# Layer 3's results turned by VectorE in 32x32 squares instead of by TensorE

## The chip, the cores and the metric

The kernel runs on one core of one Trainium2 chip. The metric is the device time of one execution in microseconds. The profile comes from one further execution that the hardware profiler recorded. Its span is shown beside the times.

## What is computed

The input x has the shape (2, 8, 256, 256): batch b, expert or channel e, row n, column d. Four blocks follow one another, each added to x: a normalisation over pairs of channels (four groups), then an expert MLP, a 3x3 convolution over channels with binarised weights, and two more expert MLPs. The MLP of an expert is what matters here:

```
h   = einsum('bend,edh->benh', gn(x), w1) + b1      # d = 256 -> h = 1024
h   = gelu(h)
out = einsum('benh,ehd->bend', h, w2) + b2          # h = 1024 -> d = 256
x   = x + out
```

There are three such layers of 8 experts (the convolution stands between the first two). The last one, whose results are the output, is called layer 3 below, after the reference.

## The kernel before

Activations lie transposed in SBUF: XT holds d on the 128 partitions (two halves c), and for each expert e and batch b the 256 rows n along the free dimension. From the second MLP layer on, the partitions hold d in an interleaved order: within each half c of 128 values, partition 2 i + g holds d = 128 c + 64 g + i, with GROUPS = 2 values of g and SPAN = 64 values of i. Every product is made in a split of three terms (high x high, high x low, low x high) for float32 accuracy, so a stationary or moving operand exists as a high part, written by ScalarE, and a low part, written by VectorE.

The three layers are 24 experts E (0 to 23), the work of one being a pass; two of them are halved, so there are 26 passes. A pass has eight units t, one for each 128 of the 1024 hidden values. In a unit TensorE makes G1 for unit u (`g1`, line 1079, six matmuls of 128x512) and then the second product of unit u - 2 (`g2`, lines 1099, 1100 and 1104, six matmuls into the ACC banks). ScalarE applies gelu to G1 (HR, line 637) and rounds it (Hh, line 641); VectorE subtracts (Hl, line 816). In between both split the weights of the next expert (lines 619 and 797, one chunk of eight in each unit), and VectorE normalises the next input (XN, line 804; Xl, line 810). At t = 2 of the next pass VectorE evicts the finished ACC banks and adds the bias and the residual (`evict`, line 830). In layer 3 this goes to XFIN, which has two slots by the parity of E. Each engine works through its own queue in order, written out by hand in one loop over the units.

XFIN holds d on partitions, but the output wants rows n on partitions. For this, in the pass after expert E of layer 3 (E from 16 to 22), TensorE transposes XFIN in four 128x128 blocks for b = 0 behind unit t = 4 and for b = 1 behind t = 6 (`out_transpose`, line 1162), into the PSUM bank TR. ScalarE copies TR to OUTT behind its t = 5 and t = 7 (`out_evac_step`, line 671), and undoes the interleaving in that copy. It waits for the store of the expert before to have left OUTT. VectorE's `evict` waits for the transposes of the expert two before (line 824). Then the SP queue stores OUTT (`store_out`, line 514), in rows of 256 values, 1 KB. In SP's queue the store for b = 0 stands behind the load of W1 of a later expert and the store for b = 1 behind the load of W2 (lines 516 to 522). The loads wait until the raw weight buffer has been split (lines 420 and 430).

The last expert (E = 23, pass FINAL) is done otherwise: `final_g2` (line 1131) makes it with rows on partitions, in two banks, one for each b. ScalarE (line 718) and VectorE (line 1014) copy them to OUTT, once the store of expert 6 from the same half of OUTT has landed, and two stores end the kernel.

Of the kernel before, what the change touches and what calls it, by code (L numbers as in the profile page):

```python
# [21 lines left out]
F32 = mybir.dt.float32  # L22
# [6 lines left out]
PART = 128  # L29
# [12 lines left out]

GROUPS = 2
SPAN = PART // GROUPS

KS = 3
ROWS = PART // C
# [54 lines left out]
def evicted_by(p):  # L102

    return DC * (p + 1)
# [147 lines left out]
def build(nc, x, w1, b1, w2, b2, cw, cb, out):  # L252
# [3 lines left out]
    with ExitStack() as ctx:  # L256
        def sb(name, shape, dt=F32, where=ctx):
            return where.enter_context(nc.sbuf_tensor(name, shape, dt))
# [4 lines left out]
        def sem(name):  # L263
            return ctx.enter_context(nc.semaphore(name))
# [57 lines left out]
            NAT = sb("NAT", [PART, NPAIR, B, 2, NC, D], F32, use)  # L322
        with ExitStack() as use:
            XFIN = sb("XFIN", [PART, 2, DC, B, N], F32, use)
            OUTT = sb("OUTT", [PART, B, NC, D], F32, use)
        XC = sb("XC", [PART, B, NBLK, NP])

        HR = sb("HR", [PART, 2, TOK])
# [32 lines left out]
        cn_done, chi, clo, conv_mm, cadded = (sem("cn_done"), sem("chi"), sem("clo"), sem("conv_mm"), sem("cadded"))  # L361
        mean_fixed = sem("mean_fixed")
        x2_in = [sem(f"x2_in{b}") for b in range(B)]
        out_tr, out_evac = sem("out_tr"), sem("out_evac")
        final_in, final_done, final_dve = sem("final_in"), sem("final_done"), sem("final_dve")
        out_st = [sem(f"out_st{b}") for b in range(B)]

# [33 lines left out]
        def evacuated(i):  # L401

            return (in_evac_dve, i // 2 - 2) if i % 2 == 0 else (in_evac_act, i // 2 + 3)

        def same_slot(p):

# [5 lines left out]
        def _(sp):  # L412
# [95 lines left out]
            def store_out(e, b, n):  # L508

                if e == C - 1 and b == B - 1:  # L510
                    sp.wait_ge(final_dve, 1)
                else:
                    sp.wait_ge(out_evac, 2 * n - 1 + b)
                sp.dma_start(out[b, e].rearrange("(c p) d -> p c d", p=PART), OUTT[:, b]).then_inc(out_st[b], 16)

            for e in range(C):
                load_w1(2 * C + e)
# [6 lines left out]
                for b in range(B):  # L524
                    store_out(e, b, e + 1)
            for b in range(B):
                sp.wait_ge(out_st[b], 16 * C)


        @block.gpsimd  # L530
# [57 lines left out]
        def _(act):  # L588
# [74 lines left out]
                    nc.scalar.dma_start(XT[GROUPS * i + g:GROUPS * (i + n):GROUPS, c, :, b],  # L663
                                        XC[j * C:(j + n) * C, b, own.stop - 1, 1:N + 1]).then_inc(x2_in[b], 16)

            def out_evac_step(E, b):

                n = E - 2 * C
                act.wait_ge(out_tr, 2 * n + b + 1)
                wait(act, out_st[b], 16 * n)  # L670
                nc.scalar.activation(OUTT[:, b].rearrange("p r (c g i) -> p (r c) g i", c=DC, g=GROUPS),
                                     TR[:].rearrange("p (a i g) -> p a g i", i=SPAN, g=GROUPS), ACT.Copy
                                     ).then_inc(out_evac, 1)

            for f in range(LAYERS):
                nc.scalar.dma_start(bias1_rows[:, f, :], b1[f].rearrange("e (t p) -> (e t) p", p=PART)
                                    ).then_inc(bias_in, 16)
# [17 lines left out]
            for u in range(UNITS):  # L695
                p, t = divmod(u, HT)
                E = PASSES[p][0]
                if u == unit(PC, 0):
                    for q in range(B * TILES):
                        conv_high(q)  # L700
                        if q >= BEHIND:
                            give_back(q - BEHIND)
                        if q == FIRST["round"]:
                            x_hi(PC, 0)
                    for q in range(B * TILES - BEHIND, B * TILES):
                        give_back(q)
                gelu(u)
                for weight in WEIGHTS_AT.get(u, ()):
                    w_hi(*weight)
                if u in SPLIT_AT:  # L710
                    x_hi(*SPLIT_AT[u])
                if E == 1 and t % 2 == 0:
                    x_evac(8 + t)
                if E > 2 * C and t in (5, 7):
                    out_evac_step(E - 1, (t - 5) // 2)
            act.wait_ge(final_done, 1)
            act.wait_ge(out_st[0], 16 * (C - 1))
            nc.scalar.activation(OUTT[:, 0].rearrange("p r d -> p (r d)"), ACC[FINAL % 2][0][:], ACT.Copy
                                 ).then_inc(out_evac, 1)


# [1 line left out]
        def _(dve):  # L723
# [95 lines left out]
            def evict(p, bs=None):  # L819
                E, bs = PASSES[p][0], bs or PASSES[p][1]  # L820
                f, e = divmod(E, C)
                dve.wait_ge(g2_done, HT * (p + 1))
                if f == LAYERS - 1:
                    wait(dve, out_tr, 2 * (E - 2 * C) - 2)
                own = slice(bs[0], bs[-1] + 1)
                cols = slice(0, width(p)) if len(bs) == len(PASSES[p][1]) else slice(bs[0] * N, (bs[-1] + 1) * N)
                for m in range(DC):
                    at = XT[:, m, e, own]
                    dst = XFIN[:, E % 2, m, own] if f == LAYERS - 1 else at
                    nc.vector.scalar_tensor_tensor(dst, acc(p, m)[:, cols].rearrange("p (b n) -> p b n", n=N),  # L830
                                                   BT2[:, f, e, m:m + 1], at, ALU.add, ALU.add).then_inc(evicted, 1)

            def add_final_bias():

# [122 lines left out]
            for u in range(UNITS):  # L957
                p, t = divmod(u, HT)
                E = PASSES[p][0]
                for J in jobs_at("aggregate", u):  # L960
                    if JOBS[J][3]["sums"] != u:
                        aggregate(J)
                if u == unit(PC, 0):
                    conv_low(0)
                    for q in range(B * TILES):
                        if q + 1 < B * TILES:
                            conv_low(q + 1)
                        conv_add(q)
                        beside_tile(q)
                if t == 2 and p > 0 and p != PC:  # L970
                    evict(p - 1)
                for J in jobs_at("sums", u):
                    if "early" in JOBS[J][3]:
                        sums(J, (1,))
                        aggregate(J)
                h_lo(u)
                for weight in WEIGHTS_AT.get(u, ()):
                    w_lo(*weight)
                for J in range(NJOBS):
                    e, bs, of, steps = JOBS[J]  # L980
                    if steps.get("early") == u:
                        sums(J, (0,))
                    if steps.get("sums") == u and "early" not in steps:
                        if u == 8:
                            for i in (7, 8):
                                dve.wait_ge(*evacuated(i))
                        sums(J)
                        if steps["aggregate"] == u:
                            aggregate(J)
                    if steps.get("mean") == u:  # L990
                        deviate(J)
                    if steps.get("eps") == u:
                        add_eps(J)
                    if steps.get("scale") == u:
                        scale_shift(J)
                        for b in range(B):
                            if J == LAST_CONV_JOB[b]:
                                to_partitions(b)
                if u + 1 in SPLIT_AT:
                    norm(*SPLIT_AT[u + 1])  # L1000
                if u in SPLIT_AT:
                    x_lo(*SPLIT_AT[u])
                if u == unit(FINAL - 1, 6):
                    add_final_bias()
                if E == 1 and t % 2 == 1:
                    x_evac(8 + t)
                if E == 1 and t == 6:
                    signs_and_means()
                    bias_of_next()
                if E == 2 and t in (2, 4, 6):  # L1010
                    band(t // 2 - 1)
            dve.wait_ge(final_done, B)
            dve.wait_ge(out_st[B - 1], 16 * (C - 1))
            nc.vector.tensor_copy(OUTT[:, B - 1].rearrange("p r d -> p (r d)"), ACC[FINAL % 2][B - 1][:]
                                  ).then_inc(final_dve, 1)


# [1 line left out]
        def _(pe):  # L1019
# [132 lines left out]
                                           xx[:, q % ring, 0:w, kh:kh + N], start=i == 0, stop=i == len(parts) - 1)  # L1152
                ins.then_inc(conv_mm, 1)

            def out_transpose(E, b):
                n = E - 2 * C
                pe.wait_ge(evicted, evicted_by(len(PASSES) - EXPERTS + E))
                wait(pe, out_evac, 2 * n + b)
                for r in range(NC):
                    for c in range(DC):  # L1160
                        at = r * D + c * PART
                        ins = nc.tensor.transpose(TR[:, at:at + PART], XFIN[:, E % 2, c, b, r * PART:(r + 1) * PART],  # L1162
                                                  ident[:])
                ins.then_inc(out_tr, 1)

            pe.wait_ge(consts, 3)
            stay_busy(5)
            for i in range(4):
# [18 lines left out]
            for u in range(UNITS):  # L1187
# [26 lines left out]
                    variance_over_partitions(J)  # L1214
                if E == 1:
                    x_transpose(8 + t)
                if E > 2 * C and t in (4, 6):
                    out_transpose(E - 1, t // 2 - 2)
            for u in (UNITS - 2, UNITS - 1):
                final_g2(u)  # L1220

# [24 lines left out]
```

## Time and profile before

| | before |
|---|---|
| median of 3 runs | 608.18 us (605.89 to 608.58) |
| profiled execution | 611.48 us, span 609.7 us |
| TensorE, matmuls | 592.4 us busy, 97% |
| VectorE | 426.7 us busy, 70% |
| ScalarE | 419.1 us busy, 69% |
| DMA, hardware queue of SP | 54262 packets, 70.31 MB, 37.9% of 16 engines |

The span is the time from the first to the last instruction of the profiled execution; the time of the execution contains it. A busy share is an average over the whole span. The profile cuts the span in 40 slices of 15.2 us; layer 3 fills the last 12 of them. A timeline row gives the start, the duration, the engine and line, and in square brackets how long the engine had been idle and what ended that.

### The profile page before, as it was taken

Reading aid. Unit: us, or ns where it says so; the run is one execution under the profiler, and the core shown is the slowest. Engines: PE = TensorE matmul, PEld = TensorE weight load, DVE = VectorE, ACT = ScalarE, POOL = GpSimd, SP = SyncE. Lnnn points to the kernel's source line nnn. Section 1 sums busy time; section 2 is a strip of 40 time slices with the busy share of each in tenths; the row PEclk is TensorE's granted clock in tenths of the full one; section 3 lists DMA queues with packets and bytes.
Section 4 is the critical chain, followed back from the end, with each engine's and each line's share of the span. In section 5 each row is a group of like instructions: output and inputs, shape, how many; then the busy total and the mean of one; then the engine's idle time right before and its main releaser. Section 6 shows DMA issues by size and latency. Waiting matters only on the chain.

```text
span 609.7 us, 8604 instructions
## 1 busy us (share of the span) xinstructions
PE 592.4 (97%) x2905; PEld 497.3 (82%) x2905; DVE 426.7 (70%) x887; ACT 419.1 (69%) x705; POOL 36.7 (6%) x57
## 2 busy tenths in 40 slices
PE   7989999999999988999999999999999999999997
PEld 7768888888889756988888888888888888888887
DVE  5885998867667977796965866866775675675632
ACT  4867767677767652687767777777777777777753
POOL 2000000000000670000000000000000000000000
PEclk9989999999999997999999999999999999999999
DMA  8843455364353393441422323223234234234001
GB/s 281 279 143 106 129 166 177 106 179 147 111 175 104 81 146 97 143 139 69 129 81 85 122 70 131 77 74 134 70 105 137 88 111 148 87 103 156 19 18 69
DMA packets 56909, 73.04 MB, mean 120 GB/s; under 512 B 4217, under 2 KB 50459, under 8 KB 56866
## 3 DMA queue, kind: packets, MB, share of 16 engines
q1 hardware_dynamic: 54262, 70.31, 37.9%
q10 hardware_dynamic: 2604, 2.19, 1.8%
q8 instruction: 23, 0.38, 0.3%
q14 instruction: 20, 0.16, 0.1%
HBM read 59.71 MB, written 8.59 MB: 112 GB/s over the span
## 4 chain that ended last, share of the span: by engine, by line
PE 85%; DMA 5%; DVE 5%; ACT 2%; issue 1%; POOL 1%; SPq 0%; ACTq 0%; DVEq 0%; POOLq 0%
PE G L1079 40%; PE ACC L1099 13%; PE ACC L1104 13%; PE ACC L1100 13%; PE ACC L1131 2%; DMA XT<-XC 1%; PE ACC L1150 1%; DVE BN L741 1%; PE TR L1162 1%; DMA W2raw<-in_L_conv_w 1%; DMA W1raw<-in_L_conv_w 1%; DMA NAT<-in_x 1%; DMA XC<-x_scratch 1%; DVE Cl L892 1%; ACT HR L637 1%
## 5 line engine op out<-in xcount | busy, mean ns | idle before, releaser
L816 DVE TENSOR_TENSOR Hl<-HR,Hh 128x512 fp32r<-128x512 f32 (+1 forms) x208 | 134.1, 645 | 157.2 <-ACT Hh L641 156.3
L637 ACT ACTIVATE HR<-G,BT 128x512 f32<-128x512 f32 (+1 forms) x208 | 136.2, 655 | 141.1 <-PE G L1079 141.0
L1079 PE MATMUL G<-Xh,W1l 128*128 128x512 f32 (+1 forms) x416 | 160.5, 386 | 0.1
L1079 PE MATMUL G<-Xh,W1h 128*128 128x512 f32 (+1 forms) x416 | 155.4, 374 | 0.0
L1079 PE MATMUL G<-Xl,W1h 128*128 128x512 f32 (+1 forms) x416 | 151.8, 375 | 0.0
L1099 PE MATMUL ACC<-Hh,W2l 128*128 128x512 f32 (+1 forms) x400 | 147.7, 373 | 0.2 <-issue 0.2
L1100 PE MATMUL ACC<-Hh,W2h 128*128 128x512 f32 (+1 forms) x400 | 147.5, 372 | 0.0
L641 ACT ACTIVATE Hh<-HR 128x512 fp32r<-128x512 f32 (+1 forms) x208 | 124.7, 600 | 6.6
L1104 PE MATMUL ACC<-Hl,W2h 128*128 128x512 f32 (+1 forms) x400 | 116.8, 373 | 0.4 <-DVE Hl L816 0.3
L1079 PEld LDWEIGHTS G<-Xh,W1h 128*128 128x128 f32 x416 | 78.6, 189 | 14.1
L1079 PEld LDWEIGHTS G<-Xh,W1l 128*128 128x128 f32 x416 | 78.7, 189 | 12.8 <-ACT HR L637 0.2
L1079 PEld LDWEIGHTS G<-Xl,W1h 128*128 128x128 f32 x416 | 78.5, 189 | 12.4 <-DVE Xl L810 0.2
L1099 PEld LDWEIGHTS ACC<-Hh,W2l 128*128 128x128 f32 x400 | 75.4, 189 | 14.0 <-issue 0.6
L1100 PEld LDWEIGHTS ACC<-Hh,W2h 128*128 128x128 f32 x400 | 75.3, 188 | 13.2
L1104 PEld LDWEIGHTS ACC<-Hl,W2h 128*128 128x128 f32 x400 | 73.0, 188 | 14.1 <-DVE Hl L816 0.8
L797 DVE TENSOR_TENSOR W1l<-W1raw,W1h 128x512 fp32r<-128x512 f32 x96 | 65.5, 685 | 2.2 <-ACT W1h L619 1.8
L797 DVE TENSOR_TENSOR W2l<-W2raw,W2h 128x512 fp32r<-128x512 f32 x96 | 66.0, 690 | 0.9 <-ACT W2h L619 0.2
L619 ACT ACTIVATE W2h<-W2raw 128x512 fp32r<-128x512 f32 x96 | 61.8, 646 | 0.3 <-DMA W2raw<-in_L_conv_w 0.3
L619 ACT ACTIVATE W1h<-W1raw 128x512 fp32r<-128x512 f32 x96 | 58.9, 616 | 2.0 <-DMA W1raw<-in_L_conv_w 2.0
L555 POOL TENSOR_TENSOR RS<-VE,half 128x2 f32<-128x2 f32 (+1 forms) x18 | 13.3, 737 | 480.2 <-DVE VE L772 480.2
L741 DVE BATCH_NORM_STATS2 BN<-XT 128x6 f32<-128x512 f32 x60 | 37.4, 681 | 3.1 <-DMA XT<-XC 3.1
L627 ACT ACTIVATE Xh<-XN 128x512 fp32r<-128x512 f32 x48 | 29.6, 619 | 11.2 <-DVE XN L804 10.7
(95 smaller groups left out, 403.4 us busy)
## 6 DMA issues: line engine op xcount, KB each, us to landing
W2raw<-in_L_conv_w SPq DMA_DIRECT2D x23, 1024.0 KB, 5.6
W1raw<-in_L_conv_w SPq DMA_DIRECT2D x34, 512.0 KB, 4.5
W1raw<-in_L_conv_w SPq DMA_DIRECT2D x7, 1024.0 KB, 5.1
XC<-x_scratch SPq DMA_DIRECT2D x16, 304.0 KB, 6.1
x_scratch<-XT SPq DMA_DIRECT2D x16, 256.0 KB
out_x<-OUTT SPq DMA_DIRECT2D x16, 256.0 KB, 2.1
NAT<-in_x SPq DMA_DIRECT2D x6, 512.0 KB, 9.2
XT<-XC SPq DMA_DIRECT2D x16, 112.0 KB
```

Of the source, the lines that this page charges most:

```text
L555: nc.gpsimd.tensor_tensor(RS[:, own], VE[:, own], half[:, own], ALU.pow).then_inc(rs_done, 1)
L619: nc.scalar.activation(dst, src, ACT.Copy).then_inc(whi, 1)
L627: nc.scalar.activation(Xh[:, par, :, b], XN[:, :, b], ACT.Copy).then_inc(xhi, 1)
L637: nc.scalar.activation(HR[:, u % 2, 0:n], G1[u % 2][:, 0:n], act_of_layer, bias=BT1[:, f, col:col + 1]).then_inc(gelu_done, 1)
L641: nc.scalar.activation(Hh[:, u % RING, 0:n], HR[:, u % 2, 0:n], ACT.Copy).then_inc(hhi, 1)
L741: nc.vector.bn_stats(BN[:, J % 2, b, i], XT[:, :, e + i, b]).then_inc(bn_done, 1)
L797: nc.vector.tensor_tensor(dst, src, high.bitcast(F32), ALU.subtract).then_inc(wlo, 1)
L816: nc.vector.tensor_tensor(Hl[:, u % RING, 0:n], HR[:, u % 2, 0:n], Hh[:, u % RING, 0:n].bitcast(F32), ALU.subtract).then_inc(hlo, 1)
L1079: ins = nc.tensor.matmul(G1[u % 2][:, 0:n], w[:, par, c, col], rhs, start=i == 0, stop=i == len(parts) - 1)
L1099: nc.tensor.matmul(acc(p, m), W2l[:, par, t, col], high, start=t == 0, stop=False)
L1100: nc.tensor.matmul(acc(p, m), W2h[:, par, t, col], high, start=False, stop=False)
L1104: ins = nc.tensor.matmul(acc(p, m), W2h[:, par, t, col], low, start=False, stop=t == HT - 1)
```

## The change

For the experts 0 to 6 of layer 3, the turn from d on partitions to n on partitions is made by VectorE. Its transpose turns each 32x32 square of a tile within the square's own 32 partitions. So XFIN is read with a stride of 8 rows: square s takes the rows n = 8 i + s for i from 0 to 31, and row n lands on partition i of each block of 32 partitions. The block k of partitions (32 k to 32 k + 31) then holds the values of d that lay on the partitions 32 k to 32 k + 31, for all rows. With the interleaving these are, in each half c and for each g, a run of 16 neighbouring values of d. The transposes sort the two values of g apart while writing, and the store of a result becomes four DMAs, one for each block k, each of 32 partitions x 32 runs of 16 values (64 bytes in DRAM; 2 KB in a row in SBUF).

The turn stands in VectorE's queue at the end of the units t = 3 (b = 0) and t = 5 (b = 1) of the next pass. TensorE's transposes, ScalarE's copies and VectorE's wait for them go. The stores keep their places in SP's queue. The last expert is stored as before.

```diff
+SQUARE = 32
+NSQ = PART // SQUARE
...
+        def stored(e):
+
+            return 16 * NSQ * e
...
-                sp.dma_start(out[b, e].rearrange("(c p) d -> p c d", p=PART), OUTT[:, b]).then_inc(out_st[b], 16)
+                if e == C - 1:
+                    sp.dma_start(out[b, e].rearrange("(c p) d -> p c d", p=PART),
+                                 OUTT[:, b].rearrange("p (c d) -> p c d", c=NC)).then_inc(out_st[b], 16)
+                    return
...
+                run = SQUARE // GROUPS
+                for k in range(NSQ):
+                    own = out[b, e, 0, run * k:run * (k + 1)]
+                    runs = bass.AP(tensor=own.tensor, offset=own.offset,
+                                   ap=[[N // SQUARE * D, SQUARE], [SPAN, N // SQUARE * D // SPAN], [1, run]])
+                    sp.dma_start(runs, OUTT[SQUARE * k:SQUARE * (k + 1), b].rearrange("p (a o) -> p a o", o=run)
+                                 ).then_inc(out_st[b], 16)
...
-            def out_evac_step(E, b):
-
-                n = E - 2 * C
-                act.wait_ge(out_tr, 2 * n + b + 1)
-                wait(act, out_st[b], 16 * n)
-                nc.scalar.activation(OUTT[:, b].rearrange("p r (c g i) -> p (r c) g i", c=DC, g=GROUPS),
-                                     TR[:].rearrange("p (a i g) -> p a g i", i=SPAN, g=GROUPS), ACT.Copy
-                                     ).then_inc(out_evac, 1)
...
-                if E > 2 * C and t in (5, 7):
-                    out_evac_step(E - 1, (t - 5) // 2)
...
-                if f == LAYERS - 1:
-                    wait(dve, out_tr, 2 * (E - 2 * C) - 2)
...
+            def turn_out(E, b):
+
+                n = E - 2 * C
+                dve.wait_ge(evicted, evicted_by(len(PASSES) - EXPERTS + E))
+                wait(dve, out_st[b], stored(n))
+                for c in range(DC):
+                    dst = OUTT[:, b].rearrange("p (s c g o) -> p c s o g", c=DC, g=GROUPS, o=SQUARE // GROUPS)[:, c]
+                    ins = nc.vector.transpose(dst, XFIN[:, E % 2, c, b].rearrange("p (i s) -> p s i", i=SQUARE))
+                ins.then_inc(out_evac, 1)
...
+                if E > 2 * C and t in (3, 5):
+                    turn_out(E - 1, (t - 3) // 2)
...
-            def out_transpose(E, b):
-                n = E - 2 * C
-                pe.wait_ge(evicted, evicted_by(len(PASSES) - EXPERTS + E))
-                wait(pe, out_evac, 2 * n + b)
-                for r in range(NC):
-                    for c in range(DC):
-                        at = r * D + c * PART
-                        ins = nc.tensor.transpose(TR[:, at:at + PART], XFIN[:, E % 2, c, b, r * PART:(r + 1) * PART],
-                                                  ident[:])
-                ins.then_inc(out_tr, 1)
...
-                if E > 2 * C and t in (4, 6):
-                    out_transpose(E - 1, t // 2 - 2)
```

## Rows read from the trace of the kernel before

**Rows 1.** The page: busy time of an engine (its share), and granted clock by slice.

```profile
PE 592.4 (97%) x2905; PEld 497.3 (82%) x2905; DVE 426.7 (70%) x887; ACT 419.1 (69%) x705; POOL 36.7 (6%) x57
...
PEclk9989999999999997999999999999999999999999
```

**Rows 2.** The chain that ended last, from 420 us on, by line.

```profile
by line: PE G L1079 45.8%; PE ACC L1099 13.8%; PE ACC L1104 13.8%; PE ACC L1100 13.7%; PE ACC L1131 6.0%; PE TR L1162 3.2%; PE ACC L1115 0.5%; DVE OUTT L1014 0.4%; PE STAT L1052 0.2%; PE STAT L1058 0.2%; issue 0.0%
```

**Rows 3.** Instructions of lines 1162 and 671: duration in ns, first and last start.

```profile
L1162 PE MATMUL TR<-ident,XFIN x56: 271/273/273, 455.1 to 600.3; 128*128 128x128 f32 x56
...
L671 ACT ACTIVATE OUTT<-TR x14: 570/581/589, 459.0 to 603.3; 128x512 f32<-128x512 f32 x14
```

**Rows 4.** Timeline of TensorE: a unit without and one with a batch (start, us).

```profile
469.72 0.39 PE L1079 MATMUL G<-Xh,W1l 128*128 128x512 f32 x1
...
472.44 0.39 PE L1079 MATMUL G<-Xh,W1l 128*128 128x512 f32 x1
...
484.33 0.60 PE L1162 MATMUL TR<-ident,XFIN 128*128 128x128 f32 x4
...
487.54 0.39 PE L1079 MATMUL G<-Xh,W1l 128*128 128x512 f32 x1
```

**Rows 5.** Timeline of TensorE in the last pass: with and without a batch.

```profile
593.91 0.60 PE L1162 MATMUL TR<-ident,XFIN 128*128 128x128 f32 x4
...
597.17 0.40 PE L1079 MATMUL G<-Xh,W1l 128*128 128x512 f32 x1
...
599.99 0.60 PE L1162 MATMUL TR<-ident,XFIN 128*128 128x128 f32 x4
```

**Rows 6.** Groups of VectorE by shape: busy us, mean ns of one, idle before.

```profile
L816 DVE TENSOR_TENSOR Hl<-HR,Hh 128x256 fp32r<-128x256 f32 x32 | 13.2, 415 | 7.3 <-ACT Hh L641 6.7
...
L884 DVE TENSOR_TENSOR band_sum<-band_tap 128x128 f32<-128x128 f32 x3 | 0.9, 291 | 0.1
```

**Rows 7.** Timeline of VectorE in the pass of expert 18, t = 3 to 5.

```profile
477.60 0.54 DVE L804 TENSOR_SCALAR XN<-XT,ST 128x512 f32<-128x512 f32 x1
478.36 0.69 DVE L816 TENSOR_TENSOR Hl<-HR,Hh 128x512 fp32r<-128x512 f32 x1 [0.22 <-ACT Hh L641]
...
481.56 0.69 DVE L816 TENSOR_TENSOR Hl<-HR,Hh 128x512 fp32r<-128x512 f32 x1 [1.30 <-ACT Hh L641]
...
484.54 0.69 DVE L816 TENSOR_TENSOR Hl<-HR,Hh 128x512 fp32r<-128x512 f32 x1 [1.69 <-ACT Hh L641]
```

**Rows 8.** Timeline of TensorE: the first reader of unit 4's Hl.

```profile
483.86 0.63 PE L1104 MATMUL ACC<-Hl,W2h 128*128 128x512 f32 x2
```

**Rows 9.** Stretches: busy us of PE, PEld, DVE, ACT, POOL; clock, DMA share, GB/s.

```profile
460.00:483.00 23.00, 23.00 (x109) 19.04 (x108) 16.62 (x32) 16.81 (x28) 0.00 (x0) 1.00 0.36 115
435.00:458.00 23.00, 23.00 (x106) 19.05 (x105) 14.49 (x28) 16.47 (x28) 0.69 (x1) 1.00 0.37 126
...
460.50:461.25 0.75, 0.75 (x6) 0.58 (x5) 0.00 (x0) 0.72 (x3) 0.00 (x0) 1.00 0.89 313
31.60:32.00 0.40, 0.40 (x4) 0.32 (x3) 0.40 (x1) 0.39 (x1) 0.00 (x0) 1.00 0.23 12
32.30:32.60 0.30, 0.30 (x3) 0.26 (x2) 0.30 (x1) 0.30 (x1) 0.00 (x0) 1.00 0.26 14
```

**Rows 10.** Timeline of SP's queue: issues, at the start and in layer 3.

```profile
26.07 5.43 SPq L451 DMA_DIRECT2D conv_rep<-in_L_conv_weight  x8
...
459.58 0.39 SPq L514 DMA_DIRECT2D out_x<-OUTT  x1
465.81 0.37 SPq L431 DMA_DIRECT2D W2raw<-in_L_conv_w  x1
...
557.84 0.39 SPq L431 DMA_DIRECT2D W2raw<-in_L_conv_w  x1
```

**Rows 11.** The page: DMA issues, KB each, median us to landing.

```profile
out_x<-OUTT SPq DMA_DIRECT2D x16, 256.0 KB, 2.1
```

**Rows 12.** Timeline of VectorE in the last pass.

```profile
597.32 0.69 DVE L816 TENSOR_TENSOR Hl<-HR,Hh 128x512 fp32r<-128x512 f32 x1 [2.57 <-ACT Hh L641]
...
606.33 0.69 DVE L1014 COPY OUTT<-ACC 128x512 f32<-128x512 f32 x1 [2.23 <-PE ACC L1131]
```

More of the change, by code:

```diff
@@ L324, in build @@
             XFIN = sb("XFIN", [PART, 2, DC, B, N], F32, use)
-            OUTT = sb("OUTT", [PART, B, NC, D], F32, use)
+            OUTT = sb("OUTT", [PART, B, NC * D], F32, use)
         XC = sb("XC", [PART, B, NBLK, NP])
@@ L363, in build @@
         x2_in = [sem(f"x2_in{b}") for b in range(B)]
-        out_tr, out_evac = sem("out_tr"), sem("out_evac")
+        out_evac = sem("out_evac")
         final_in, final_done, final_dve = sem("final_in"), sem("final_done"), sem("final_dve")
@@ L526, in _ @@
             for b in range(B):
-                sp.wait_ge(out_st[b], 16 * C)
+                sp.wait_ge(out_st[b], stored(C - 1) + 16)
         @block.gpsimd
@@ L713, in _ @@
                     x_evac(8 + t)
-                if E > 2 * C and t in (5, 7):
-                    out_evac_step(E - 1, (t - 5) // 2)
             act.wait_ge(final_done, 1)
-            act.wait_ge(out_st[0], 16 * (C - 1))
-            nc.scalar.activation(OUTT[:, 0].rearrange("p r d -> p (r d)"), ACC[FINAL % 2][0][:], ACT.Copy
+            act.wait_ge(out_st[0], stored(C - 1))
+            nc.scalar.activation(OUTT[:, 0], ACC[FINAL % 2][0][:], ACT.Copy
                                  ).then_inc(out_evac, 1)
@@ L1012, in _ @@
             dve.wait_ge(final_done, B)
-            dve.wait_ge(out_st[B - 1], 16 * (C - 1))
-            nc.vector.tensor_copy(OUTT[:, B - 1].rearrange("p r d -> p (r d)"), ACC[FINAL % 2][B - 1][:]
+            dve.wait_ge(out_st[B - 1], stored(C - 1))
+            nc.vector.tensor_copy(OUTT[:, B - 1], ACC[FINAL % 2][B - 1][:]
                                   ).then_inc(final_dve, 1)
```

## The prediction

> **What bounds the kernel now.** I read the page's busy times and clock first. TensorE is busy 592.4 of 609.7 us, at full granted clock from the first slices on, while VectorE has 30% of the span free [rows 1]. So what leaves TensorE's queue shortens the run, if nothing else becomes late. The chain of waits, read from 420 us on, says it more sharply: it is TensorE nearly throughout, and the transposes of line 1162 are 3.2% of that stretch [rows 2]. There are 56 of them, in 14 batches of four, and 14 copies on ScalarE (line 671) that empty them [rows 3]. The reader is to see that the copies are not on that chain and the transposes are.
>
> **What is removed.** A TensorE instruction's duration overlaps its neighbours, so I price a batch by the pitch of the unit that contains it. A plain unit lasts from 469.72 to 472.44, 2.72 us; one with a batch from 484.33 to 487.54, 3.21 us [rows 4]. The difference is 0.49 us, more than the 0.44 us of the batch itself, since the first matmul behind it is slower. In the last pass a unit with a batch takes 597.17 - 593.91 = 3.26 us and one without it 599.99 - 597.17 = 2.82 us, so 0.44 us [rows 5]. Twelve batches stand in passes 17 to 22 and two in the last: 12 x 0.49 + 2 x 0.44 = 6.8 us, all on the path. The 14 copies of 0.58 us leave ScalarE, off the path: nothing.
>
> **What is added on VectorE.** Each turn is two transposes of 128x256 float32, behind the subtractions of t = 3 and t = 5. No transpose of VectorE is in the trace. The nearest row by size is 128x256 at 0.415 us; 128x128 takes 0.29 us, so 128 more columns cost 0.12 us [rows 6]. I take 0.415 us each, 0.8 us a turn; the lower end is 0.3 us, the upper end a rate four times slower, 0.17 + 8 x 0.12 = 1.1 us, so 2.3 us a turn. What hides it: in the fullest stretch, pass 18 at t = 3, VectorE ends XN at 478.14 and has 0.22 us free before Hl of unit 4 [rows 7]. That Hl would end 0.6 us later, at 479.7 instead of 479.05, or 2.1 us later at the upper end, and TensorE first reads it at 483.86 [rows 8]. Then come gaps of 1.30 us and of 1.7 us. So nothing, up to 2.3 us a turn. A pass lasts 23.0 us, 22.0 without its two batches. Two turns add 1.7 us (4.6 at the upper end) to the 16.6 us that VectorE works in it [rows 9]: it fits. The wait on line 824 goes; it was never late.
>
> A wait moves with the work: VectorE now waits until the previous store from the same OUTT half has landed; before, ScalarE did. Behind it on VectorE stands the next Hl, and TensorE waits for that. For b = 1 the store is issued behind the W2 load at about 466.2 and is wanted again at about 482.5, some 16 us later [rows 7, 10].
>
> **What is added on the queues.** This is where the change can be lost. A store was one DMA of 256 runs of 1 KB. Now it is four DMAs of 32 partitions x 32 runs of 64 bytes: 4096 runs. 14 stores of 16 become so; expert 7 keeps its form. They share SP's queue with the weight loads. Let X be the time that the DMA engines need for one store. The three nearest rows [rows 9]: (a) The old store: a share of 0.89 over 0.75 us on 16 engines, 10.7 us for 256 packets, so 42 ns a packet of 1 KB. (b) One small load of line 451, 128 packets of 36 bytes: 0.23 x 0.40 x 16 = 1.5 us, so 11.5 ns each; the next gives 0.26 x 0.30 x 16 = 1.25 us, 9.8 ns. (c) The same load in wall time: 128 packets in 0.3 to 0.4 us, although the engines were but a quarter busy. By (b) X = 4096 x 11.5 / 16 = 2.9 us. By (a), if a run cost as much whatever its length, X = 4096 x 42 / 16 = 10.7 us; by (c), if that pace were a limit on handing packets out, X = 4096 x 0.35 / 128 = 11.2 us. The bounds are 2.9 and 11.2 us. I take 4 us: the size is nearest to (b), with something added because (b) reads DRAM and this writes it.
>
> What X is allowed: in a pass of 23.0 us the engines work 0.36 x 23.0 = 8.3 us, of which two old stores are 1.3 (2 x 10.7 / 16), so its pair of weight loads needs 6.9 us [rows 9]. 22.0 - 6.9 = 15.1 us are free for two stores: up to X = 7.5 us no load comes late, in the steady state. At 4 us there is no backlog, and the stores land long before VectorE's wait. SP issues 8 short instructions a pass where it issued two: at 0.6 to 0.7 us each (eight took 5.43 us), 2.7 us a store [rows 10]. A store 0 stands ahead of the W2 load but is issued four units before it; store 1 stands ahead of W1, also four units away. That fits without cost.
>
> **The tail.** The last turned store (expert 6, b = 1) must land before VectorE may write OUTT again after the last matmul. Without the batch of t = 4, Hl of the last pass's unit 5 would end at 598.01 - 0.44 = 597.6 on the old clock [rows 12], the turn at 598.4, the first of its DMAs would start to move about 0.9 us after its issue (459.58 to 460.5, [rows 9, 10]), at 599.3. The last matmuls end at 606.33 - 0.9 = 605.4 [rows 12]. With about 1 us from the last data to the semaphore, from the old store's 2.1 us to landing less its 0.9 and most of its data time [rows 11], X may be 5 us. At X = 4, nothing; above 5, X - 5.
>
> The sum: 609.7 - 6.8 = 602.9 us of span, 604.7 us for the profiled execution, which took 611.5. Against the median of 608.2 us of the runs shown that is 601.4 us; the profiled one is 3.3 us above that median, so I carry the difference over, not the level.
>
> A rule of the Trainium skill speaks against the change, and nothing above rests on it. The shortest rows read, 36 bytes, cost 10 to 12 ns [rows 9], and no row shows a short write. "DMA: Bandwidth & Descriptors", Specifications, says that line rate wants at least 512 bytes and that below them a DMA reads, modifies and writes. If that doubles (b), an estimate, X is 5.8 us and the time 602.2 us instead of 601.4, the second rival; if it costs more, it is the first.
>
> **The rivals.** *The short runs fill the DMA engines.* From about 457 us (pass 17's t = 3, 478.14 - 23.0, a turn and 0.9 us more) the 14 turned stores and nine weight loads (SP's queue has five of W2 and four of W1 from 465.81 to 557.84 us [rows 10]: 4.5 pairs of 6.9 us, 31 us) must pass one queue by the end of the last matmuls, 605.4 - 12 x 0.49 = 599.5 us with all batches gone, less 1 us. That leaves 141 - 31 = 110 us, 7.9 us a store. Beyond this each us of X costs 14 us: it comes back as loads that ScalarE waits for and as VectorE's wait on the store. The old time is reached at X = 7.9 + 6.8 / 14 = 8.4 us, 33 ns a run, and from there the time is 608.2 + 14 (X - 8.4): 631 us at X = 10, 647 us at 11.2. For it: (a) and (c), and that every run is a write to DRAM. Against it: the small packets that are there take 10 to 12 ns. Chance 0.27, the slower side almost alone.
>
> *The tail alone grows.* X between 5 and 7.9 us: 601.4 + (X - 5), to 604.3 us. Chance 0.12.
>
> *VectorE becomes the bound.* If one transpose takes 2 us, four are 8 us on top of 16.6 in one pass and 14.5 in the other kind [rows 9], 23.6 us on average against 22.0: 1.6 us in each of six passes, 601.4 + 9.6 = 611 us. It decides where this eats the 6.8 us, from 1.9 us a transpose. Against it: that is over four times the nearest row. Chance 0.04.
>
> *The gain is given back on TensorE.* The freed 0.49 us become waits for Hh or Hl, as ScalarE's and VectorE's work of a unit is unchanged: 607 to 608 us. Against it: ScalarE and VectorE wait for TensorE and not the reverse (the gap before Hl is 1.3 us in [rows 7]). Chance 0.07.
>
> **How the numbers follow.** Forecast 601.4 us, chance 0.50. A median of this kernel can tell about 0.5%, 3 us, from no change. Faster by more than that: 0.50 + 0.12 = 0.62, less 0.02 for a partial give-back in these, 0.60. Within: 0.07 + 0.02 and the corner of the first rival near X = 8.4, 0.10. Slower: the rest of that rival and VectorE, 0.30. The low end is the forecast less 2 us for the spread of the runs, 599.5. The high end must reach into the first rival: X = 10 us, 631 us, leaves out some 0.17 above. The forecast's own range is 599.5 to 604.
>
> **What would show it.** Line 1162 is gone from TensorE and the pitch at t = 4 and 6 is 2.72 us; the transposes on VectorE last 0.3 to 1.1 us; the DMA share of a pass rises from 0.36 to about 0.68 at X = 4 (6.9 + 8 of 22.0 us) and is near 1 in the rival; W1h and W2h then wait for DMA, and TensorE for Hl or Hh. A DMA wait before OUTT at the end, or in front of the turns, shows X above the limits. I am wrong first of all if a 64-byte write costs over 33 ns of an engine.

## The result, and the profile after

| | before | changed |
|---|---|---|
| median of six runs each | 606.25 us (603.22 to 608.58) | 599.91 us (597.40 to 607.34) |
| ratio | | 0.9885, 95% interval 0.9843 to 0.9927 |
| profiled execution | 611.48 us, span 609.7 | 607.34 us, span 605.4 |

The changed kernel is faster by 1.15%, 7.0 us of 606.25; the forecast was 6.8. The ratios of this document leave out disturbed executions, of which the changed kernel's six hold one, the profiled one; without it its median is 598.6 us. So the level was missed: 598.6 us lies below the 599.5 that the range began with.

The page of the changed kernel: busy times, granted clock and SP's DMA queue ([rows 1] are those of before).

```profile
PE 586.6 (97%) x2849; PEld 491.8 (81%) x2849; DVE 442.1 (73%) x915; ACT 412.4 (68%) x691; POOL 36.5 (6%) x57
...
PEclk9999999999999997999999999999999999999999
...
q1 hardware_dynamic: 108694, 70.31, 42.2%
```

TensorE has 56 instructions fewer, VectorE 28 more, and the queue moves the same 70.31 MB in twice the packets.

The chain that ended last, from 420 us on, by line (answers [rows 2]):

```profile
by line: PE G L1098 47.8%; PE ACC L1123 14.4%; PE ACC L1118 14.4%; PE ACC L1119 14.4%; PE ACC L1150 6.2%; PE ACC L1134 0.5%; DVE OUTT L1033 0.4%; PE STAT L1071 0.2%; PE STAT L1077 0.2%; issue 0.0%
```

It is TensorE again, with only the transposes gone; nothing came in their place. All waits from 451 to 605 us, of more than a moment (engine and line, what for, us in total, times, longest):

```profile
POOL RS L575 <- DVE VE L781: 86.7, 2, 43.3
ACT HR L657 <- PE G L1098: 44.6, 54, 1.9
DVE Hl L825 <- ACT Hh L661: 39.1, 36, 2.5
ACT OUTT L727 <- PE ACC L1150: 2.2, 1, 2.2
DVE OUTT L1033 <- PE ACC L1150: 2.2, 1, 2.2
```

TensorE stands on the right side only, and no line names a DMA: no load and no store is waited for. VectorE's last copy still waits for TensorE.

The turns, on VectorE's timeline in the pass of expert 18 (answers [rows 7]):

```profile
479.22 0.54 DVE L813 TENSOR_SCALAR XN<-XT,ST 128x512 f32<-128x512 f32 x1
479.67 1.28 DVE L847 STREAM_TRANSPOSE OUTT<-XFIN 128x256 f32<-128x256 f32 x2
480.83 0.67 DVE L825 TENSOR_TENSOR Hl<-HR,Hh 128x512 fp32r<-128x512 f32 x1
...
483.90 1.26 DVE L847 STREAM_TRANSPOSE OUTT<-XFIN 128x256 f32<-128x256 f32 x2
485.66 0.69 DVE L825 TENSOR_TENSOR Hl<-HR,Hh 128x512 fp32r<-128x512 f32 x1 [0.49 <-ACT Hh L661]
```

A turn takes 1.27 us; its second transpose starts 0.6 us after the first. The gap of 1.30 us that [rows 7] show ahead of the next Hl is used up by the delay, and 0.49 us of idle time remain further on. The Hl of unit 4 ends at 481.50. The matmuls that read it start on TensorE at 484.98, 3.5 us later:

```profile
484.75 0.39 PE L1119 MATMUL ACC<-Hh,W2h 128*128 128x512 f32 x1
484.98 0.61 PE L1123 MATMUL ACC<-Hl,W2h 128*128 128x512 f32 x2
485.43 0.39 PE L1098 MATMUL G<-Xh,W1l 128*128 128x512 f32 x1
```

**A yardstick.** The ratios below have intervals of some 0.4% to each side, since the first 240 us of an execution vary: in the 13 profiles the first eviction into XFIN starts anywhere from 441.2 to 451.6 us. What lies behind the convolution is steady: from VectorE's first eviction there to the first one into XFIN it is 189.3 us in both profiles. I therefore also read in every profile the stretch from the first eviction into XFIN to VectorE's copy of the last ACC bank to OUTT. These are the two ends before (the last number pair of the first line is the first and last start), and after:

```profile
L830 DVE SCALAR_TENSOR_TENSOR XFIN<-ACC,BT,XT x14: 739/743/749, 448.9 to 586.5; 128x512 f32<-128x512 f32 x14
...
L1014 DVE COPY OUTT<-ACC x1: 692/692/692, 606.3 to 606.3; 128x512 f32<-128x512 f32 x1
```

```profile
L837 DVE SCALAR_TENSOR_TENSOR XFIN<-ACC,BT,XT x14: 739/743/747, 451.5 to 583.1; 128x512 f32<-128x512 f32 x14
...
L1033 DVE COPY OUTT<-ACC x1: 691/691/691, 602.1 to 602.1; 128x512 f32<-128x512 f32 x1
```

It is 606.3 - 448.9 = 157.4 us before and 602.1 - 451.5 = 150.6 us after: 6.8 us, the forecast to a tenth. The two profiled spans differ by only 4.3 us, because the stretch began 2.6 us later in the changed one (451.5 against 448.9); the 604.7 us that were forecast for the profiled execution became 607.34 by that.

### The profile page after: what moved, and what is told of

Read it like the earlier page. It is cut to its first block, busy times and chain, and to the rows that moved or that the text cites. A ratio compares the mean times of both kernels' runs of the same rounds, so it can differ in the third digit from the quotient of the medians.

```text
span 605.4 us, 8530 instructions
## 1 busy us (share of the span) xinstructions
PE 586.6 (97%) x2849; PEld 491.8 (81%) x2849; DVE 442.1 (73%) x915; ACT 412.4 (68%) x691; POOL 36.5 (6%) x57
## 3 DMA queue, kind: packets, MB, share of 16 engines
q1 hardware_dynamic: 108694, 70.31, 42.2%
## 4 chain that ended last, share of the span: by engine, by line
PE 85%; DMA 6%; DVE 5%; ACT 2%; issue 1%; POOL 1%; SPq 0%; ACTq 0%; DVEq 0%; POOLq 0%
PE G L1098 41%; PE ACC L1118 13%; PE ACC L1119 13%; PE ACC L1123 13%; DMA W1raw<-in_L_conv_w 2%; PE ACC L1150 2%; DMA XT<-XC 2%; PE ACC L1169 1%; DVE BN L750 1%; DMA NAT<-in_x 1%; DMA XC<-x_scratch 1%; DVE Cl L909 1%; ACT HR L657 1%; DVE W1l L806 1%; DVE XC L917 1%
## 5 line engine op out<-in xcount | busy, mean ns | idle before, releaser
L647 ACT ACTIVATE Xh<-XN 128x512 fp32r<-128x512 f32 x48 | 29.6, 618 | 11.2 <-DVE XN L813 10.7
```

The costliest lines, as they stand in the source:

```text
L647: nc.scalar.activation(Xh[:, par, :, b], XN[:, :, b], ACT.Copy).then_inc(xhi, 1)
```

## The experiments

All are the changed kernel with one thing altered. "Stretch" is the yardstick, read in one profile of each. A ratio is to executions of the kernel before that were made beside the run: their medians are 607.8 us for e1 to e4, 605.5 for e5 to e8 and 606.6 for e9 to e11, each group on another chip. So compare ratios and stretches across the groups, not medians.

| run | what is altered | stretch, us | median, us | ratio to before, 95% |
|---|---|---|---|---|
| before | | 157.4 | 606.3 | |
| changed | | 150.6 | 599.9 | 0.9885 (0.9843 to 0.9927) |
| e1 | TensorE's 14 batches back | 157.5 | 607.9 | 1.0024 (0.9985 to 1.0062) |
| e2 | stores in runs of 1 KB | 150.6 | 603.4 | 0.9926 (0.9888 to 0.9964) |
| e3 | nothing | 150.6 | 603.7 | 0.9921 (0.9881 to 0.9962) |
| e4 | turns two units later | 154.3 | 603.4 | 0.9950 (0.9908 to 0.9993) |
| e5 | runs of 8 values | 153.1 | 603.1 | 0.9966 (0.9928 to 1.0005) |
| e6 | runs of 4 values | 368.6 | 817.0 | 1.3504 (1.3454 to 1.3554) |
| e7 | a spare turn behind each | 150.6 | 599.5 | 0.9899 (0.9861 to 0.9937) |
| e8 | two spare turns behind each | 151.3 | 599.6 | 0.9929 (0.9894 to 0.9964) |
| e9 | 8 idle steps in the convolution | 150.6 | 600.0 | 0.9898 (0.9861 to 0.9934) |
| e10 | 30 idle steps there | 150.6 | 603.4 | 0.9947 (0.9924 to 0.9970) |
| e11 | nothing | 150.6 | 600.8 | 0.9889 (0.9844 to 0.9933) |

**Does the gain come from TensorE's queue alone? (e1)**

```diff
+            def out_transpose(E, b):
+                pe.wait_ge(evicted, evicted_by(len(PASSES) - EXPERTS + E))
+                for r in range(NC):
+                    for c in range(DC):
+                        at = r * D + c * PART
+                        ins = nc.tensor.transpose(TR[:, at:at + PART], XFIN[:, E % 2, c, b, r * PART:(r + 1) * PART],
+                                                  ident[:])
+                ins.then_inc(out_tr, 1)
...
+                if E > 2 * C and t in (4, 6):
+                    out_transpose(E - 1, t // 2 - 2)
```

(VectorE's wait for these transposes at its evict is back too; nobody empties TR, and TensorE waits for nobody to.)

> The changed kernel with TensorE's 14 batches of four transposes put back behind t = 4 and t = 6, into the bank TR that nobody reads; ScalarE's copies stay away, VectorE's turns and the short runs stay. Theory (the whole gain is what left TensorE's queue, 14 x 0.49 us): level with the kernel before, ratio 0.998 to 1.002, 7 us slower than the changed kernel. Rival (ScalarE's copies or the moved wait gave part of the gain): 1 to 4 us faster than the kernel before.

The stretch is 600.3 - 442.8 = 157.5 us, that of before, and the ratio is level. ScalarE's copies are absent and VectorE's turns are present here, and e7 below shows that more turns cost nothing, so the one does not hide the other: the batches are the whole gain.

**Do the short runs cost? (e2)** The values of the first seven experts stand in another order in DRAM.

```diff
-                for k in range(NSQ):
-                    ...
+                sp.dma_start(out[b, e].rearrange("(c p) d -> p c d", p=PART),
+                             OUTT[:, b].rearrange("p (c d) -> p c d", c=NC)).then_inc(out_st[b], 16)
```

> The changed kernel with expert 0 to 6 stored in one DMA of 256 runs of 1 KB, as before, so that the values in DRAM stand in another order than the reference's. Theory (the short runs are hidden by the engines' free time): the same as the changed kernel within 1 us, 7 us below the kernel before. Rival (the stores, whose issues fill SP for 4 to 6 us each, cost at the end or in loads): 1 to 3 us faster than the changed kernel.

Nothing, to 0.1 us of the stretch, and the ratio is that of e3. What the short runs take is time of the DMA engines that was free. A pass in this run, and one with the short runs (DMA share next to last):

```profile
446.00:468.00 22.00, 22.00 (x99) 18.25 (x98) 18.11 (x32) 16.20 (x27) 0.00 (x0) 1.00 0.38 120
```

```profile
455.50:477.50 22.00, 22.00 (x100) 18.25 (x99) 18.11 (x33) 16.20 (x27) 0.00 (x0) 1.00 0.53 120
```

**The same kernel again (e3, e11).** No edit.

> The changed kernel once more, for the level and its spread. If the gain is 6.8 us and the level of both kernels moves from run to run with what happens ahead of layer 3 (granted clock, first loads), the ratio to the kernel before is 0.988 to 0.990, and the spans of the runs follow their mean granted clock, about 595 us at 0.999 and 605 us at 0.991. If the gain was over-read from few runs, the ratio is 0.993 or more.

> The changed kernel once more on the same chip, beside the two: 6.8 us below the kernel before at equal granted clock, spans of 595 us at a mean clock of 0.999 to 605 us at 0.991; the first turn's eviction to VectorE's last copy takes 150.6 us again.

The ratio was 0.9921 on one chip and 0.9889 on another, the first less than I expected and the second within; the stretch was 150.6 us both times. What moves the ratio lies ahead of the stretch, not in the change.

**Is the end tight? (e4)**

```diff
-                if E > 2 * C and t in (3, 5):
-                    turn_out(E - 1, (t - 3) // 2)
+                if E > 2 * C and t in (5, 7):
+                    turn_out(E - 1, (t - 5) // 2)
```

(The ScalarE copy at the end gets a semaphore of its own, final_act.)

> The changed kernel with VectorE's turns two units later, behind t = 5 and t = 7. Theory (a store takes 4 to 6 us to be issued and must land before OUTT is written again at the end): the last turned store is issued from about 601 to 605 us instead of 595.4 to 598.9, lands at about 607, and VectorE's last copy waits for it: 4 to 6 us slower than the changed kernel, 1 to 3 us faster than before. Rival (the end is not tight): no more than 1 us slower than the changed kernel.

The stretch grew by 3.7 us, a little under the 4 to 6 expected, and VectorE's last copy waits for the store, as in the next run:

```profile
DVE OUTT L1035 <- DMA out_x<-OUTT: 4.9, 1, 4.9
```

That the turns stand at t = 3 and 5 is what keeps the end free.

**What may a store cost? (e5, e6)** The runs are cut, the values stay in place.

```diff
-                run = SQUARE // GROUPS
+                run, part = SQUARE // GROUPS, 8        # 4 in e6
                 for k in range(NSQ):
-                    own = out[b, e, 0, run * k:run * (k + 1)]
+                    for h in range(run // part):
+                        own = out[b, e, 0, run * k + part * h:run * k + part * (h + 1)]
...
+                        src = OUTT[SQUARE * k:SQUARE * (k + 1), b].rearrange("p (a o) -> p a o", o=run)
+                        sp.dma_start(runs, src[:, :, part * h:part * (h + 1)]).then_inc(out_st[b], 16)
```

> Each of the four DMAs of a store is cut in two, of 1024 runs of 8 values (32 bytes) each: eight DMAs, 8192 runs a store. The output is the same. Theory by engine time (9.4 ns a run of 64 bytes, about 8 ns for 32): X = 4.1 us, nothing in the passes. Theory by issue (SP's four issues took 4.2 to 5.9 us, some 1.0 to 1.5 us for 1024 runs): 8 to 12 us a store, the last one lands some 4 us too late, and the passes are near their limit of 7.5 us: 4 to 40 us slower than the changed kernel. My formula from 8.4 us on gives the time of the kernel before at 8.4 us and 14 us more for each us.

> The same with runs of 4 values (16 bytes): sixteen DMAs, 16384 runs a store. By engine time alone, at 8 ns, X = 8.2 us, about the time of the kernel before. By issue, 17 to 22 us a store: 14 x (17 - 8.4) = 120 us and more above the kernel before. The two runs together tell whether a run costs the same whatever its length and what a store may take.

The page of each: SP's queue (packets, MB, share of 16 engines), e5 first.

```profile
q1 hardware_dynamic: 166934, 70.32, 46.1%
```

```profile
q1 hardware_dynamic: 283414, 70.32, 71.8%
```

Shares times spans give the queue's engine time: 0.379 x 609.7 = 231 us before, 0.422 x 605.4 = 255 us changed, 0.461 x 598.6 = 276 us for e5, 0.718 x 814.4 = 585 us for e6. All but the 14 turned stores is 231 - 14 x 0.67 = 222 us. So a store takes X = 2.4 us in runs of 64 bytes (9.4 ns a run), 3.9 us in runs of 32 (7.6 ns), and 25.9 us in runs of 16 (25 ns). Cutting the run to 32 bytes leaves the price of a run.

The 25 ns are a mean, and not what a run of 16 bytes takes by itself. Added up packet by packet from e6's trace, X is 23.8 us, as the loads took longer there too. Nine in ten of these runs took 7 to 9 ns, like those of e5, and one in twenty took 125 ns or more. The first store of e6 shows how it begins (DMA share and GB/s are the last two numbers; the share adds the times of the packets, and passes 1 where they overlap):

```profile
453.00:454.00 1.00, 1.00 0.53 18
...
456.00:462.00 6.00, 1.00 1.53 13
```

At first 18 GB/s, 1125 runs in a us, take 0.53 x 16 = 8.5 us of the engines, 7.5 ns each. In the six us from 456 on it is over 30 ns each, and fewer of them pass. SP's queue slows down with it, and issues without a pause from 449 to 805 us:

```profile
449.02 21.49 SPq L535 DMA_DIRECT2D out_x<-OUTT  x16
470.55 1.40 SPq L439 DMA_DIRECT2D W2raw<-in_L_conv_w  x1
472.00 26.01 SPq L535 DMA_DIRECT2D out_x<-OUTT  x16
```

Whether it is the length of the runs or the number of DMAs in the queue at once that brings the long packets, no run tells.

With runs of 8 the passes lose nothing and the end 2.5 us. VectorE waits there 4.7 us for the store, which SP needs 6.6 to 9.6 us to issue. That is between the two theories on record: engine time alone would have cost nothing, and by issue I had expected 4 us and more. With runs of 4 the whole machine goes at the queue's pace, in the way the first rival described:

```profile
DVE OUTT L848 <- DMA out_x<-OUTT: 178.3, 12, 21.8
...
PE ACC L1124 <- DVE Hl L826: 109.2, 10, 16.3
ACT HR L658 <- DVE Hl L826: 95.8, 6, 18.6
ACT W2h L640 <- DMA W2raw<-in_L_conv_w: 68.0, 5, 15.0
```

VectorE waits in front of its turns for the store before, the Hl behind them is late, and TensorE waits for it. The rival's rule was 14 us for each us of X above 7.9. The stretch grew by 368.6 - 150.6 = 218 us, which asks for X = 7.9 + 218 / 14 = 23.5 us, against 23.8 from the packets and 25.9 from the page. The rule fits this one point, and so would one by SP's issue time, 21.5 to 26.0 us a store. The price of a 64-byte run that would have set it off is not there.

**What may VectorE's turns cost? (e7, e8)**

```diff
+                for again in range(1):        # 2 in e8
+                    for c in range(DC):
+                        nc.vector.transpose(SPARE[:, b, again, c].rearrange("p (s g o) -> p s o g", g=GROUPS,
+                                                                           o=SQUARE // GROUPS),
+                                            XFIN[:, E % 2, c, b].rearrange("p (i s) -> p s i", i=SQUARE))
                 ins.then_inc(out_evac, 1)
```

> Each of VectorE's turns is followed by a second one of the same data into a spare tile: 2.5 us a turn. VectorE then works 18.1 + 2.5 = 20.6 of 22.0 us in the fuller kind of pass. Theory (VectorE has 3 us of slack before a subtraction is wanted by TensorE): 0 to 1 us slower than the changed kernel. Rival (the slack is less than 1.3 us): 14 x 1 us slower.

> Two spare turns behind each: 3.8 us a turn, VectorE 23.1 of 22.0 us in the fuller pass and 22.0 in the other. It is over its limit: TensorE waits for Hl, some 1 us a fuller pass for the whole and more where the work is bunched, 3 to 10 us slower than the changed kernel. If it is still level, VectorE's slack is larger than its busy time says.

One spare turn costs nothing. Two cost 0.7 us in all, less than I expected, though VectorE is then busy for whole passes (third engine column, after PE and PEld):

```profile
452.50:474.50 22.00, 22.00 (x100) 18.24 (x99) 21.97 (x40) 16.06 (x26) 0.00 (x0) 1.00 0.54 120
474.50:496.50 22.00, 22.00 (x99) 18.02 (x98) 21.17 (x45) 15.97 (x26) 1.67 (x1) 1.00 0.54 120
```

The fuller kind of pass is full, the other has 0.8 us free. My sum for e8 took 1.27 us for each further turn. They follow closely and overlap, so it is less. e7's row of the fuller kind:

```profile
455.50:477.50 22.00, 22.00 (x100) 18.26 (x99) 20.18 (x36) 16.20 (x27) 0.00 (x0) 1.00 0.54 120
```

That is 20.18 - 18.11 = 2.07 us more for two spare turns. Four ask for 18.11 + 4.14 = 22.25 us, 0.25 above the 22.0 of a pass. Three such passes give the 0.7 us; on TensorE's own timeline three pitches are longer, by 0.18, 0.23 and 0.28 us.

**What moves the level? (e9, e10)** `stay_busy` makes matmuls of 128x128 on TensorE that nobody reads.

```diff
                         if q == FIRST["mean"]:
+                            stay_busy(8)        # 30 in e10
                             mean_over_partitions(FIRST_JOB)
```

> The changed kernel with eight idle matmuls of 128x128 (about 1.0 us together) on TensorE in the middle of the convolution, just ahead of its wait for the statistics of the first expert of layer 2. It asks what sets the level: in some profiled executions TensorE waits 5.2 us there, for gathered rows that VectorE needs, and the granted clock then falls to half for 3 to 10 us; in others it waits 1.4 us and keeps it. Theory (the clock falls because TensorE is idle so long): a shorter idle time of 4.2 us makes the fall rarer or leaves it, the level is the same within 1 us. Nothing is lost in the good executions, since 1.0 us fits in the 1.4.

> The same with thirty idle matmuls, 3.8 us. In an execution where the wait is 5.2 us it leaves 1.4 us idle. Theory (idle time is what takes the clock): no stretch of half clock in the convolution in any profile, clocks of 0.996 and more, the slowest executions 3 us faster than the changed kernel's slowest (about 604 instead of 607), the fastest 2.4 us slower (about 600 instead of 597.4), the spread smaller. Rival (the clock falls with the slow transfers and not with the idle time): half clock still there, and everything 2.4 us slower.

In the convolution TensorE waits for the statistics of layer 2's first expert, and these wait on VectorE for rows given back by DMA. In the profile of the changed kernel:

```profile
227.42 0.86 PE L1169 MATMUL TR<-Cl,BAND 128*128 128x512 f32 x3
233.45 0.59 PE L1071 MATMUL STAT<-MV,ones_mean 128*128 128x1 f32 x2 [5.17 <-DVE MV L765]
```

```profile
231.41 1.29 DVE L750 BATCH_NORM_STATS2 BN<-XT 128x6 f32<-128x512 f32 x2 [3.63 <-DMA XT<-XC]
```

The granted clock around it (the third number from the end; the DMA share follows it):

```profile
228.00:230.00 2.00, 0.28 (x2) 0.00 (x0) 0.00 (x0) 0.96 (x2) 0.77 (x1) 1.00 0.90 142
230.00:232.00 2.00, 0.00 (x0) 0.00 (x0) 0.59 (x1) 0.09 (x1) 0.00 (x0) 1.00 0.92 99
232.00:234.00 2.00, 0.55 (x3) 0.55 (x3) 1.86 (x7) 0.00 (x0) 0.00 (x0) 0.66 0.59 101
234.00:236.00 2.00, 2.00 (x6) 1.61 (x6) 1.60 (x5) 0.00 (x0) 0.00 (x0) 0.50 0.20 64
236.00:240.00 4.00, 4.00 (x12) 3.19 (x12) 1.67 (x4) 0.82 (x1) 1.48 (x2) 0.57 0.39 114
```

The clock falls to half, 1.2 GHz, still in the idle time (by the row of 232 to 234 at about 232.6, and the first matmul starts at 233.45), and is half for 2 x (0.34 x 2 + 0.50 x 2 + 0.43 x 4) = 6.8 us, 6.0 of them with work. In e1's profile the same wait is 1.4 us and the clock stays at 1.00. The other profiles agree: with this wait at 4.7 to 6.1 us (before, changed, e3, e7, e8) half clock came with it for 3.4 to 10.2 us, with 1.2 to 2.2 us (e1, e2, e4, e5, e6, e9, e11) it did not. The transfers differ from 216 to 226 us. This is the changed kernel, then e1 (SP's columns: clock, DMA share, GB/s):

```profile
216.00:226.00 10.00, 1.00 1.00 141
```

```profile
216.00:226.00 10.00, 1.00 0.61 158
```

More bytes took less engine time there. I mis-sized the idle steps: one is two matmuls, and 30 of them last 6.9 us, not 3.8. With them TensorE is never idle at this place. The clock stays whole there, although the transfers of this execution were of the slow kind (compare the changed kernel's row). That is against the rival, by which the clock falls with the slow transfers:

```profile
216.00:226.00 10.00, 1.00 0.97 141
```

None of its 12 runs had a mean clock under 0.996, where three of e3's 12 were at 0.986 to 0.992 and four at 0.994. The spans went from 599.7 to 603.4 us, 3.7 us apart, against 595.5 to 605.4 for the six of the changed kernel. So at this place the idle time takes the clock, as expected. But 6.9 us of idle work cost more than they save: the median is 2.6 us above that of e11, which ran beside it. Eight steps, 1.95 us, cost nothing that I can tell and gain nothing.

The length of the idle time is not the whole rule. At about 40 us TensorE waits 1.8 to 2.7 us in every profile; half clock for 3.4 us followed in eight of them (before, changed, e1, e2, e3, e7, e10, e11) and not in the other five, e6 with the longest wait, 2.7 us, among them. What decides there is open.

## Why the prediction was right, and where it was not

**The gain.** 14 batches at 0.49 and 0.44 us, 6.8 us: shown by the stretch and by e1. TensorE's passes of layer 3 follow one another in 21.76 and 22.25 us, where they took 22.76 and 23.25: the two batches of a pass. Pricing a batch by the pitch of its unit, and not by its four instructions, was what made it exact.

**VectorE's turns.** Nothing, as predicted; the size was off. A transpose lasts 0.69 us and a turn 1.27 us, against 0.415 and 0.8 of the sum and an upper end of 1.1 and 2.3. The nearest row by size, a subtraction, was two fifths too low. The margin claimed, up to 2.3 us a turn, was there: with e7's spare turns it is 2.4 us on VectorE each time, and they cost nothing.

**The stores.** X was to be 4 us between bounds of 2.9 and 11.2. It is 2.4 us of engine time, under the lower bound, and the DMA share of a pass is 0.53 where 0.68 was forecast. The bound by pace (c), 11.2 us a store, does not hold for these larger DMAs. By the clock on the wall a store takes longer than X, and this was missed: SP needs 3.7 to 5.9 us to issue four such DMAs, not 2.7 us. The median of one is the 0.67 us of the forecast, but in most stores one or two of the four take far longer (duration in ns, lowest, median, highest):

```profile
L533 SPq DMA_DIRECT2D out_x<-OUTT x56: 570/667/2583, 458.2 to 598.3; - x56
```

At the end that is what counts. The last turned store was released at 595.37 us, its data ended between 600 and 601 us, and VectorE wanted OUTT at 602.06 (the changed kernel; clock, DMA share, GB/s):

```profile
599.00:600.00 1.00, 1.00 0.79 96
600.00:601.00 1.00, 1.00 0.24 28
601.00:602.00 1.00, 1.00 0.00 0
```

So the end held by 1 to 2 us, and e4 and e5 went through it.

**The rule of the Trainium skill** ("DMA: Bandwidth & Descriptors", Specifications: a read-modify-write below 512 bytes) set neither 5.8 us nor more. Runs of 64 bytes at 9.4 ns and of 32 at 7.6 ns show no such cost here: they are no dearer than the 36-byte reads at 9.8 to 11.5 ns that the sum started from. Whether the engines read before they wrote, no row tells. At 16 bytes the mean is 23 to 25 ns, but most runs still took 7 to 9, so a price of that kind on every short write is not what e6 shows.

**The rivals.** The first did not occur; its chain of waits is shown by e6, and its slope fits there in one point. The tail's wait is shown by e4 and e5, but not its condition: e5, with an X of 3.9 us, under the limit of 5, lost 2.5 us at the end. The time to issue counts there, not X. VectorE as the bound: e8 stands at the edge of it. That TensorE would give the gain back did not happen.

**The level and the range.** Here the prediction failed: 601.4 us and a low end of 599.5. The step was "the low end is the forecast less 2 us for the spread of the runs". Three runs of before, 605.9 to 608.6, had stood for the kernel's spread and middle. In the 35 runs beside e1 the spans of before go from 601.6 to 610.9 us, ordered by mean granted clock: 602.3 us in the middle of the eight at 0.999 and 1.0, 610.2 in the middle of the five at 0.991 and 0.992. The first three runs lay in the middle and upper part, so a later median came out 1.9 us lower without any change. That is most of the 2.8 us between 601.4 and 598.6; the rest is where the changed kernel's own few executions fell. The same kernel's median was 603.7 us in e3 and 600.8 in e11, both inside the range, so which side of 599.5 a median of six falls on is in part luck. Like with like, the change is what was forecast: at 0.999 and 1.0 the spans beside e7 are 602.1 us before (11 runs), and 595.2, 595.2 and 595.5 for e7, 6.9 us less. The span of before that the forecast was made against, 609.7 us at a clock of 0.991, had the stretch of half clock in the convolution, the 7 in the sixteenth slice, and another of 3.4 us, the 8 in the third [rows 1]. I called that "at full granted clock from the first slices on". The changed kernel's profile, at 0.991 too, had both as well. Why the transfers of the convolution stage go slower in some executions is open.

## What to carry to other kernels

Work that can leave a full TensorE's queue for an engine with gaps is worth the pitch of the unit that it leaves, if the new work is placed where the next product of that engine is wanted late. Count a store in short runs by what the queue has free in a pass, and at the end by the time that its issues take. For the level, read what the granted clock and the waits ahead of the change do from run to run. A range about a median of three runs has to be as wide as these make it.

## What the runs showed of the hardware

- A transpose of 128x256 float32 in 32x32 squares on VectorE, read with a stride of 8 values and written in runs that alternate, lasts 0.69 us, 0.6 us from one to the next. A subtraction of 128x512 takes as long.
- In writes to DRAM a run of 64 bytes takes 9.4 ns of a DMA engine and one of 32 bytes 7.6 ns. Runs of 16 bytes, sixteen DMAs of 1024 in a row, took 7 to 9 ns in nine of ten cases, but 23 to 25 ns on average, and SP needed 21.5 to 26.0 us to issue the sixteen of a store.
- SP issued four DMAs of 1024 runs of 64 bytes in 3.7 to 5.9 us: 0.67 us is the median of one, 2.58 us the longest. Of the DMAs of 256 runs of 1 KB in e2 the median is 0.38.
- In the convolution TensorE's clock was granted at half, 1.2 GHz, for 3.4 to 10.2 us in the five profiles where TensorE was idle for 4.7 to 6.1 us; it fell before the idle time ended or just as it did. With 1.2 to 2.2 us idle it stayed whole. With idle matmuls over that place it was whole in the profile of e10, and the mean clocks of its twelve runs, 0.996 and more, leave no room for a stretch of 6.8 us (a loss of 3.4 us, 0.6% of the span).
- Early in the kernel, after 1.8 to 2.7 us idle, the clock was half for 3.4 us in eight of 13 profiles and whole in five.
